# Segment sums of a state-space scan: one float32 matmul each, or two float32r matmuls over high and low halves

## The reference, cut to what matters

```
dt = softplus(proj + dt_bias);  dA = dt * (-exp(A_log))          # 1024 tokens x 64 heads
c = cumsum(dA, within a chunk of 32)
L[t, s] = exp(c[t] - c[s])  for s <= t                            # per head and chunk
Y_diag[t] = sum over s of (C[t].B[s]) * L[t, s] * x[s] * dt[s]
Y_off[t]  = exp(c[t]) * C[t] . state at the chunk's start
y = (Y_diag + Y_off + D * x) * silu(z);  out = rmsnorm(y) @ out_proj
```

## Time and profile before

| | |
|---|---|
| median of 3 runs | 737.68 us (734.25, 737.68, 737.98) |
| the profiled execution, its own time | 735.4 us |
| its span from first to last instruction | 733.6 us |
| mean granted TensorE clock | 0.887 of 2.4 GHz |
| busy: PE, DVE, ACT, POOL | 572.9, 403.4, 375.1, 153.5 us |
| the eight tiles of the scan | about 375 to 500 us of the span |

### The profile page before, as it was taken

One profiled execution on the slowest core, in us unless ns is written; L12 is line 12 of the kernel. 1 busy time (PEld: TensorE's weight loads), 2 busy tenths in 40 slices (PEclk: granted clock), 3 DMA queues, 4 the chain that ended last, 5 costly groups with the idle time before them and its releaser, 6 DMA issues.

```text
span 733.6 us, 14233 instructions
## 1 busy us (share of the span) xinstructions
PE 572.9 (78%) x5820; PEld 434.9 (59%) x5822; DVE 403.4 (55%) x586; ACT 375.1 (51%) x799; POOL 153.5 (21%) x121
## 2 busy tenths in 40 slices
PE   0176967578767766669999999987489999999990
PEld 0043645445545642445555665656389999999990
DVE  5889899679897377955745554524611111211113
ACT  6986878449876507654666555553212222222212
POOL 1000000000001028621058544300012223222210
PEclk9995588785888998898999999998579999999996
DMA  9400000000001000000000000000498888988815
GB/s 355 150 1 1 1 1 1 1 1 0 1 2 30 1 0 1 0 1 1 2 2 4 2 2 3 2 3 30 152 361 311 330 331 304 333 332 313 339 51 179
DMA packets 18480, 72.18 MB, mean 98 GB/s; under 512 B 4528, under 2 KB 9776, under 8 KB 14704
## 3 DMA queue, kind: packets, MB, share of 16 engines
q1 hardware_dynamic: 15120, 64.19, 23.9%
q0 software_dynamic: 2208, 6.03, 2.1%
q10 hardware_dynamic: 1088, 1.05, 0.4%
HBM read 66.16 MB, written 5.11 MB: 97 GB/s over the span
## 4 chain that ended last, share of the span: by engine, by line
PE 59%; DVE 22%; ACT 11%; issue 4%; DMA 2%; POOL 1%; SPq 0%; ACTq 0%; DVEq 0%; POOLq 0%
PE PS L1348 48%; DVE nmx L991 3%; DVE arena L904 3%; DVE arena L901 3%; ACT arena L591 2%; PE PS L1401 2%; PE PS L1386 1%; PE PS L1599 1%; PE PS L1417 1%; ACT arena L578 1%; DVE A L923 1%; PE PS L1464 1%; DMA arena<-ypair 1%; ACT arena L751 1%; DVE arena L1095 1%
## 5 line engine op out<-in xcount | busy, mean ns | idle before, releaser
L1348 PE MATMUL PS<-arena 128*128 128x128 f32 (+5 forms) x1682 | 194.1, 290 | 17.4 <-DVE arena L1095 10.1
L1348 PEld LDWEIGHTS PS<-arena 128*128 128x128 f32 (+3 forms) x1684 | 162.3, 170 | 43.0 <-issue 25.7
L1322 DVE TENSOR_TENSOR R<-arena,PS 128x128 f32<-128x128 f32 x23 | 6.6, 288 | 135.1 <-ACT arena L832 135.1
L591 ACT ACTIVATE arena<-PS,nmx 128x128 f32<-128x128 f32 (+1 forms) x128 | 52.2, 425 | 44.4 <-DVE nmx L991 44.4
L1401 PE MATMUL PS<-ident,arena 128*128 128x128 f32 x192 | 38.6, 357 | 32.6 <-ACT arena L578 30.5
L1348 PE MATMUL PS<-arena,R 128*128 128x256 f32 x276 | 63.5, 380 | 0.6 <-ACT arena L838 0.6
L1348 PEld LDWEIGHTS PS<-arena,R 128*128 128x128 f32 x276 | 50.6, 190 | 6.9 <-issue 0.9
L1401 PEld LDWEIGHTS PS<-ident,arena 128*128 128x128 f32 x192 | 30.2, 186 | 39.9 <-ACT arena L591 25.9
L462 POOL DMA_INDIRECT ypair<-arena,oid x23 | 22.8, 991 | 135.9 <-ACT arena L838 135.9
L372 POOL TENSOR_SCALAR arena<-ident,gcol 128x128 f32<-128x128 f32 x4 | 2.4, 603 | 233.2 <-DMA gcol<-in_gcol 233.2
L432 POOL TENSOR_TENSOR arena<-arena 128x1024 f32<-128x1024 f32 x16 | 37.8, 2369 | 40.5 <-DVE arena L1177 32.5
(11 more groups left out here) (271 smaller groups left out, 1130.1 us busy)
## 6 DMA issues: line engine op xcount, KB each, us to landing
arena<-in_moe SPq DMA_DIRECT2D x23, 1408.0 KB, 6.7
arena<-in_moe SPq DMA_DIRECT2D x23, 768.0 KB
inproj<-in_inproj SPq DMA_DIRECT2D x1, 1344.0 KB, 10.6
arena<-in_fT SPq DMA_DIRECT2D x1, 1024.0 KB, 5.1
xT<-in_xT SPq DMA_DIRECT2D x1, 1024.0 KB, 5.5
R<-in_w1T SPq DMA_DIRECT2D x1, 1024.0 KB, 7.5
R<-in_w2T SPq DMA_DIRECT2D x1, 1024.0 KB, 9.5
R<-in_w3T SPq DMA_DIRECT2D x1, 1024.0 KB, 11.6
```

What stands on the lines that cost most here:

```text
L591: sc.activation(pr[u % 2][:, j, 0:n], PS[:, 2 * (u % 2) + j // 2, (j % 2) * 256:(j % 2) * 256 + n], ACT.Exp, bias=nmx[:, u % 2, j:j + 1], ...
L1348: last = mm(dst, l, r, start=(n == 0), stop=(n == len(pairs) - 1))
```

## The change

The steps `dA` are cut into `dAh` (a copy of `dA` written as float32r) and `dAl` (`dA - dAh`, written as float32r). GpSimd builds `stp` from `dAh`; VectorE builds the same products for `dAl`, in a new `lower_steps(i)` of two tensor_tensors of 128x1024 each, into two pairs of buffers that lie over `dmats` and `A`. Each segment is then two matmuls with float32r operands, one over `stp` and one over `lower`, added up in PSUM; the first four decay sums likewise over `dAh` and `dAl`. ScalarE makes float32r copies of `ugt` and `gtf` (128x128 each). A counter `dve_stp` tells TensorE that the lower products are there. `lower_steps(0)` stands in front of VectorE's convolution, `lower_steps(1)` behind `front(0)`, and `lower_steps(i + 2)` behind `front(i + 1)`.

```
 # GpSimd
-pool.tensor_tensor(stp[i % 2], dA[:, i, :].unsqueeze(2).broadcast_to([P, SH, Q]),
+pool.tensor_tensor(stp[i % 2][:], dAh[:, i, :].bitcast(F).unsqueeze(2).broadcast_to([P, SH, Q]),
                    step[:].unsqueeze(1).broadcast_to([P, SH, Q]), ALU.mult).then_inc(S["pool_stp"], 1)
 # ScalarE, behind the scaling of outproj
+sc.activation(ugtr[:], ugt[:], ACT.Copy).then_inc(S["act_opw"], 1)
+sc.activation(gtfr[:], gtf[:], ACT.Copy).then_inc(S["act_opw"], 1)
 # VectorE, in front of the convolution
-done(v.tensor_tensor(dA, dt, anegb..., ALU.mult), "dve_dt")
+done(v.tensor_tensor(dA, dt, anegb..., ALU.mult))
+done(v.tensor_copy(dAh[:], dA), "dve_dt")
+done(v.tensor_tensor(dAl[:], dA, dAh[:].bitcast(F), ALU.subtract), "dve_dt")
+def lower_steps(i):
+    if i >= 2:
+        dve.wait_ge(S["pe_seg"], 4 * (i - 1))
+    each = [P, SH // 2, Q]
+    for l in range(2):
+        done(v.tensor_tensor(lower[i % 2][l][:], dAl[:, i, 32 * l:32 * l + 32].bitcast(F).unsqueeze(2).broadcast_to(each),
+                             step[:].unsqueeze(1).broadcast_to(each), ALU.mult), "dve_stp")
+lower_steps(0)
...
 front(0)
 dve.wait_ge(S["act_gate"], NT)
+lower_steps(1)
 for i in range(NT):
     if i:
         gated(i - 1)
     if i >= 2:
         add_out(i - 2)
     if i + 1 < NT:
         front(i + 1)
+    if i + 2 < NT:
+        lower_steps(i + 2)
 # TensorE
-last = acc(PS[0:m, b, :], [(gtf[0:m, 0:m], dA[0:m].rearrange("p i h -> p (i h)"))])
+last = acc(PS[0:m, b, :], [(gtfr[0:m, 0:m], w[0:m].rearrange("p i h -> p (i h)")) for w in (dAh, dAl)])
...
-pe.wait_ge(S["dve_dt"], 1)
+pe.wait_ge(S["act_opw"], XT + 2)
+pe.wait_ge(S["dve_dt"], 2)
...
 def segments(i, q):
     pe.wait_ge(S["pool_stp"], i + 1)
+    pe.wait_ge(S["dve_stp"], 2 * i + 1 + q // 2)
...
-    acc(bank(q % 2), [(ugt[:], stp[i % 2][:, 16 * q:16 * q + 16, :]...)], "pe_seg")
+    acc(bank(q % 2), [(ugtr[:], w.rearrange("p h t -> p (h t)")) for w in
+                      (stp[i % 2][:, 16 * q:16 * q + 16, :], lower[i % 2][q // 2][:, 16 * (q % 2):16 * (q % 2) + 16, :])],
+        "pe_seg")
```

More of the change, by code:

```diff
@@ L66, in at, with next_at, placed @@
             return v
+        def next_at():
+            return (nc.sbuf_base + 31) // 32 * 32
+        def placed(name, at, words, shape, dt):
+            return nc.alloc_sbuf_tensor_at(name, shape, dt, offset=at + 4 * words)
         xT = sb("xT", [P, CT, N])
+        A_at = next_at()
         A = sb("A", [P, CT, N])
+        R_at = next_at()
         R = sb("R", [P, 4, NCH, CT * HALF])
@@ L85, in build @@
         wu = sb("wu", [P, 4, 2, CT])
+        inproj_at = next_at()
         inproj = sb("inproj", [P, CT, PROJ])
@@ L124, in build @@
         sums = [arena[:, w:w + K] for w in range(8 * K, 12 * K, K)]
-        ekq, ekvq = arena[:, 12 * K:13 * K], sb("ekvq", [P, N])
+        ekq = arena[:, 12 * K:13 * K]
+        ekvq_at = next_at()
+        ekvq = sb("ekvq", [P, N])
         tiny = sb("tiny", [P, 2])
+        dmats_at = next_at()
         dmats = [sb(f"dmat{i}", [P, N]) for i in range(2)]
@@ L174, in build @@
         lm = [wide(0), wide(2 * K)]
-        stp = [wide(4 * K), spent[:, 512:512 + 2 * K].rearrange("p (h t) -> p h t", h=SH)]
+        stp = [placed(f"stp{i}", at, w, [P, SH, Q], FR) for i, (at, w) in enumerate(((arena_at, 4 * K), (inproj_at, 512)))]
         xbd = [wide(12 * K + 512).rearrange("p h (c q) -> p h c q", c=NC), wide(14 * K + 512).rearrange("p h (c q) -> p h c q", c=NC)]
+        lower = [[placed(f"lower{i}{l}", at, l * K, [P, SH // 2, Q], FR) for l in range(2)] for i, at in enumerate((dmats_at, A_at))]
+        dAh = placed("dAh", ekvq_at, 512, [P, NT, SH], FR)
+        dAl = placed("dAl", R_at, 2 * 2 * K + 3 * 512, [P, NT, SH], FR)
+        ugtr = placed("ugtr", arena_at, 29 * K + 512, [P, P], FR)
+        gtfr = placed("gtfr", arena_at, 29 * K + 512 + P, [P, P], FR)
         es = arena[:, 6 * K:6 * K + 512].rearrange("p (c i h) -> p c i h", c=NC, i=NT)
@@ L196, in build @@
         anegb = sb("anegb", [P, SH])
-        def placed(name, words, shape, dt):
-            return nc.alloc_sbuf_tensor_at(name, shape, dt, offset=arena_at + 4 * words)
         ring = arena[:, 0:RING * EW].rearrange("p (r n) -> p r n", r=RING)
@@ L279, in build @@
             act_hgt act_rs dve_dec act_decay pool_pad dve_rinv pe_r act_rT dve_num act_ekq act_ekvq act_sq act_yw
-            dve_hqt dve_iden dve_msq dve_peak pe_rows pe_ss pool_diag pool_osc pool_root""".split()
+            dve_hqt dve_iden dve_msq dve_peak pe_rows pe_ss pool_diag pool_osc pool_root dve_stp""".split()
         S = {n: sem(n) for n in NAMES}
@@ L1147, in _ @@
             done(v.scalar_tensor_tensor(dt, dt, 0.0, ut.rearrange("p (i h) -> p i h", i=NT), ALU.max, ALU.add))
-            done(v.tensor_tensor(dA, dt, anegb[:].unsqueeze(1).broadcast_to([P, NT, SH]), ALU.mult), "dve_dt")
+            done(v.tensor_tensor(dA, dt, anegb[:].unsqueeze(1).broadcast_to([P, NT, SH]), ALU.mult))
+            done(v.tensor_copy(dAh[:], dA), "dve_dt")
[8 more added lines that the diff above has]
+            lower_steps(0)
             for n in range(6):
@@ L1639, in segments @@
                     pe.wait_ge(S["act_seg"], 4 * i + q - 1)
-                acc(bank(q % 2), [(ugt[:], stp[i % 2][:, 16 * q:16 * q + 16, :].rearrange("p h t -> p (h t)"))], "pe_seg")
+                acc(bank(q % 2), [(ugtr[:], w.rearrange("p h t -> p (h t)")) for w in
+                                  (stp[i % 2][:, 16 * q:16 * q + 16, :], lower[i % 2][q // 2][:, 16 * (q % 2):16 * (q % 2) + 16, :])],
+                    "pe_seg")
             def state(i, c):
@@ L1705, in output @@
                     pe.wait_ge(S["dve_x"], X_FFN + i)
-                if i == 0:
-                    pe.wait_ge(S["act_opw"], XT)
                 acc(PS[:, 3, 0:P], [(ones[:], sqT[i % 2][:, l * P:(l + 1) * P]) for l in range(XT)])
```

## The result

The changed kernel takes 746.65 us (median of 4 runs, 745.48 to 747.19) against 736.99 for the kernel before (4 runs). The ratio is 1.0135, 95% interval 1.0104 to 1.0166: 1.35% slower, more than the 0.5% that the prediction set as its bound. Forecast were 740 and a range of 729 to 746.

A forecast was written before the change was run, and what follows sets the result against it. TensorE was taken to bound the scan, GpSimd its start too. Tiles 0, input stage +0.9 and clock +1.6 made +2.5 on 735.4; with the runs' median 2.3 above that, about 740, range 729 to 746.

The forecast's parts named there:

- the likeliest case: Tiles: VectorE's products and GpSimd's instructions alternate on the path to SBUF; 42%, 737 to 744 with its clock.
- the term of the clock: TensorE behind two waits of 4.2 us: low clock may cost 1.6 each, counted once.
- The pass: TensorE's segments: a float32r pass takes 0.24 us, so a segment costs 0.48 instead of 0.91.
- The rival in which a pass takes 0.45: Segments: float32r pass as long as a float32 half, no segment shorter; +5 or 6, 743; 10%.
- The shared path: VectorE's two-SBUF-operand products and GpSimd exclude each other; in odd rounds TensorE stands 4.2 us, costing 8.4 in all.
- The rival in which VectorE keeps the path for both products: Odd rounds: second product follows before GpSimd steps in, ending 1.0 late; 733; 22%.
- The even rounds: First product ahead of the mask, second behind it; tokens nearly on time, 0.3 for each of two rounds.
- The rival for this, 14% and 744: Both waits' clock at 1.6, a third in tile 1's start with about 2 more waiting; +6, 744; 14%.
- The start of the tiles: Four products of 1.2 alternate with a full GpSimd, half beside TensorE's own waits: some 2 us lost.
- The input stage: Before the tiles: copy, subtraction and tile 0's products make the convolution 7.0 late, its last taps 0.9 late.
- everything is hidden: Tiles: products and GpSimd don't meet, through a late mask or drifting stages; -11 - 1.7, 725; 12%.
- the forecast for the tiles: Scan: -11 saved by segments, +8.4 odd rounds, +0.6 even rounds, +2 start, making 0; clock 1.6 added separately.

The follow-up runs named there:

- experiment 6: Three more 256-column matmuls before tile 0's first state, added to the changed kernel with 4 long matmuls filling TensorE's waits before tokens 3 and 5: 739.69 us.
- high half alone: Changed kernel without VectorE's products, its segments multiplying only the high half of the steps: 728.52 us, ratio 0.9879 to the kernel before.
- 20 short matmuls: Changed kernel with 20 unread matmuls of 96 columns in each of TensorE's waits before tokens 3 and 5: 743.46 us.
- 4 long ones: Changed kernel with 4 unread matmuls of 512 columns in each of TensorE's waits before tokens 3 and 5: 739.54 us.

## Why the prediction was wrong

The mechanism was right, and the likeliest case was the one that came. The step that failed is the term of the clock: "Two waits of 4.2 may each cost that; I count one", 1.6 us. Both waits brought the low clock, and each cost about twice the 1.6 (3.5 and 3.2). Together they measured 6.4 to 7.1 us. The range's upper bound was added up from the same 1.6.

- *The pass.* 0.24 forecast, 0.23 measured. The rival in which a pass takes 0.45 falls.
- *The shared path.* Taking turns was forecast from single instructions and came row for row: `gated` 6.93 us behind the end of `front` (406.85) where F + 7.5 was forecast, tokens at F + 11.3 (F + 12.0), the waits 3.83 and 3.81 (4.2). The third odd round's wait is 0.52, as no `steps` is left there. The rival in which VectorE keeps the path for both products falls: `steps` got in between.
- *The even rounds.* 13.20 in place of 14.77 and 14.78, 1.6 shorter; 1.3 was forecast. The forecast had the second mask between the two products, but they were over (423.28 to 425.76) before it began (426.15).
- *The clock.* I priced it by a stretch of 3.40 us, as if the low clock always lasted that long. Behind tokens it lasted 7.40 and 6.80, with TensorE busy in nearly all of it, so that close to half of it was lost. And the choice to count one of two equal waits had no row behind it. The rival for this, 14% and 744, had the right mechanism, and the same small price.
- *The start of the tiles.* The sum had 2 us of loss against 3.1 of shorter segments up to tile 2's first state (8 of the 28 that share the 11), so -1.1; it is +1.6. This error of 2.7 is the other part of the miss. The term that was too small is the "some 2 us" of products alternating with GpSimd: half of them were to lie beside TensorE's own waits, but VectorE works through this stretch all but without a pause, and TensorE ends up waiting for it (experiment 6). The clock falls there too, yet moving its fall did not move tile 2.
- *The input stage.* +0.9 forecast, +1.1 measured. Behind the convolution the products are 2.2 us cheaper than that (37.25 in place of 39.46).
- *The rival "everything is hidden".* It was priced at -11 in the tiles (the prediction's own terms make 12.1, 13.8 less 1.7, with which its forecast would have been 739), and the runs where it holds show -6.0 and -6.4. Only the rounds from tile 2 on give what a segment saves; with the high half alone an odd round (from tile 2's first state to tile 3's) gives 2.0 and an even one 0.6, where TensorE then stands 1.36 in `turn` without a releaser.

In sum, against the forecast for the tiles: the two waits -0.8, the clock +5.1 (3.5 and 3.2, less 1.6), the start +2.7, together +7.0. The table has +9.1 where +1.6 was forecast, 7.5 more; the 0.5 left is spread over the other rounds.

## What to carry to other kernels

Before new VectorE work goes into a gap, look at what GpSimd does in it: if the new instruction has two operands in SBUF, the two engines may take turns for whole instructions, as they did here, and moving one small operand to PSUM can decide the sign of the change. Price a new wait on TensorE as wait plus what its low clock will take from the dense work behind it, not by the length of some other slow stretch; matmuls that nobody reads, put into the wait, show that price by itself. A saving on the busiest engine counts only in those rounds where it is also the one that ends last.

## What the runs showed that I had not expected

- VectorE's products beside GpSimd: 1.22 us in fourteen of fourteen with an operand in PSUM, up to 4.54 with both in SBUF.
- A float32r matmul of 512 columns starts 0.23 us behind the last one; the float32 pair takes 0.91, about four times that. The Trainium skill's "FP8 and Floating Point Precision", section TensorE Precision Notes, has four passes for float32, and this agrees.
- The low clock followed a wait of 1.41 us but not another of the same kind in the same kernel, and keeping TensorE busy in a wait moved it in one kernel and removed it in another. The runs don't say what decides it.
- Waits of TensorE without a releaser in the profile came and went with the code (1.92 us with the 20 short matmuls, none there with the 4 long ones). Their cause stays open.
